# Moving the turn of the attention output one pipeline step later, and the score mask from the end of a step to just before its scores

## The chip, the cores and the metric

One core of a Trainium2 chip runs the whole program. The metric is the device time in microseconds (us), as the median of several runs; lower is better.

## The reference, cut to what matters

```python
x = x + L0(x, cond_512)   # modulated linear, attention over 16 heads within each token, modulated linear
x = x + L1(x, cond_512)   # low-rank linear map made from cond_512
x = x + L2(x, cond_512)   # modulated linear
x = x + L3(x, ids, cond)  # layer norms with gathered gains, six blocks through a 3072 -> 512 -> 512 MLP
```

`x` is 2 x 2048 tokens of 512 numbers. Only L0 is touched by the change:

```python
kx = modulated_linear(x, s, k_aff_w, k_aff_b, k_w, k_b).reshape(B, N, H, D)   # H = 16, D = 32
scores = einsum('bnhd,bnjd->bnhj', kx, kx) / sqrt(D)                          # 16 x 16 for each token
out = einsum('bnhj,bnjd->bnhd', softmax(scores), kx).reshape(B, N, F)
out = modulated_linear(out, s, o_aff_w, o_aff_b, o_w, o_b)
```

## The kernel before, in words

The 4096 tokens are 32 tiles of 128 (T = 32). L0 is a software pipeline: in step s each engine works on several tiles at once, in an order written out by hand in one function `attend(s, has)` for each engine; `has(k)` is true where tile s - k exists. `prepare(s)` follows each `attend(s)` and holds one-time work (weights, tables, low-rank factors). A list in `order` mixes the last steps (s from T to T + 7) with the first work of the later layers. All engines run their queues in order and wait on semaphores. `nth(MIX, "back", t + 1)` names a count of a semaphore that several links of one chain raise in turn: for the mixing chain "back" (VectorE), "styled" (GpSimd), "turned" (TensorE).

For tile t the work goes so:

- step t - 1: GpSimd multiplies the loaded tile by the style (`x_in`, L1668), ScalarE rounds it (`xh`, L1035), VectorE takes the rest (`xl`, L1324).
- step t: TensorE makes the keys in 12 products (`ps_k`, L663); VectorE scales (`kb`, L1298), GpSimd adds the bias (`kb`, L1685), VectorE turns 32 x 32 blocks (`kt`, L1309). At the end of its queue of step t + 1 TensorE writes a mask of large negative numbers into the score bank (`ps_s`, L681, one product of `mask_lr` and `mask_rr`, 128 rows of which two are not zero), for the tile whose scores come in the next step.
- step t + 1: ScalarE spreads the keys into a block diagonal (`k_diag`, L994).
- step t + 2: TensorE turns the keys into values (`ps_vt`, L634) and adds the scores onto the mask (`ps_s`, 32 products, L639). VectorE: `mx` (L1267), `low` (L1271); ScalarE `e` (L1021); VectorE `total` (L1287), `rinv` (L1291); GpSimd multiplies `e` by `rinv` (L1679); VectorE turns it into `at` (L1304); ScalarE spreads it (`at_diag`, L994).
- step t + 3: TensorE mixes the values (`ps_v`, L652, 32 products). VectorE turns the result into `om` (L1278) right after `low` of the next tile and before its `total`; GpSimd multiplies `om` by the second style (L1675); TensorE turns `om` at the end of its queue (`ps_t`, L702, 4 transposes).
- step t + 4: ScalarE rounds it at the head of its queue (`oh`, L1005, function `high_o`), VectorE takes the rest at the head of its own (`ol`, L1257, `low_o`), ahead of `mx`.

From step 8 on, TensorE makes one output block per step out of a finished group of four tiles (`ps_o`, 12 products, L604). SyncE loads its residual (`xb`, L468), GpSimd adds a bias to it (`xb`, L1662), VectorE adds the product (`xb`, L1319). In odd steps 5 to 19 TensorE also makes part of the decoder rows (`ps_u`, L691), in later steps table and fold products. GpSimd's order in a step is: residual bias, `x_in`, `om`, `e`, `kb`.

The wait of TensorE that both the old and the new order have ahead of the mixing product (before its first `ps_v` of a step) is:

```python
                    if later(t, 1):
                        pe.wait_ge(mix_step, nth(MIX, "back", t))
```

it holds the bank `ps_v` until VectorE has turned the tile before.

Of the kernel before, what the change touches and what calls it, by code (L numbers as in the profile page):

```python
# [5 lines left out]
F32 = mybir.dt.float32  # L6
F32R = mybir.dt.float32r
# [181 lines left out]
def body(nc, sems, I, A, M, ident, cond, style_t, demod_t, wv, table_t, u_dram, a_dram, x1_dram, out):  # L189
# [46 lines left out]
    with ExitStack() as ctx:  # L236
# [376 lines left out]
        def _(pe):  # L613
# [13 lines left out]
            def attend(s, has):  # L627
                if has(2):
                    t, p = s - 2, s % 2
                    pe.wait_ge(k_step, nth(KEYS, "turned", t + 1))  # L630
                    if later(t, 1):
                        pe.wait_ge(v_ready, t)
                    for m in range(PR // Q):
                        mm = nc.tensor.transpose(ps_vt[:, m, :], kt[p][:, Q * m:Q * m + Q, :].rearrange("p g h -> p (g h)"), ident[:, :])  # L634
                    mm.then_inc(v_turned, 1)
                    pe.wait_ge(k_diag_ready, t + 1)
                    for j in range(PR):
# [37 lines left out]
                if has(1):  # L675
                    if later(s, 2):
                        pe.wait_ge(softmax_step, nth(SOFTMAX, "low", s - 1))
                    else:
                        pe.wait_ge(mask_ready, 2)
                        pe.wait_ge(diag_zero, 3)  # L680
                    nc.tensor.matmul(ps_s[:, :, :], mask_lr[:, :], mask_rr[:, :], start=True, stop=False, skip_group_check=True)  # L681
# [12 lines left out]
                if has(3):  # L694
                    t = s - 3
# [286 lines left out]
        def _(act):  # L982
# [24 lines left out]
            def attend(s, has):  # L1007
                if has(4) and s != T + 3:
                    high_o(s - 4)
# [32 lines left out]
                if s == T + 2:  # L1042
                    high_o(T - 1)
# [179 lines left out]
        def _(dve):  # L1223
# [35 lines left out]
            def attend(s, has):  # L1259
                if has(4) and s != T + 3:  # L1260
                    low_o(s - 4)
# [63 lines left out]
                if s == T + 2:  # L1325
                    low_o(T - 1)
# [24 lines left out]
            def prepare(s):  # L1351
                m = slice(0, MLP_ROWS)
                if s == -1:
                    dve.wait_ge(consts_in, 16 * 4)
                    nc.vector.tensor_copy(mask_lr[0:2, :], at[0:2, 0:4, :].rearrange("p a b -> p (a b)")).then_inc(mask_ready, 1)
                    nc.vector.tensor_copy(mask_rr[0:2, :], e[0:2, :, :].rearrange("p a b -> p (a b)")).then_inc(mask_ready, 1)
# [290 lines left out]
        def _(pool):  # L1647
            nc.gpsimd.memset(mask_lr[:, :].bitcast(F32), 0.0)
            nc.gpsimd.memset(mask_rr[:, :].bitcast(F32), 0.0)
# [7 lines left out]
            def attend(s, has):  # L1657
                if has_o(s):
                    n = s - O_AT
                    fo = n % G  # L1660
                    pool.wait_ge(res_landed[n % 3], 16 * (n // 3 + 1))
                    nc.gpsimd.tensor_scalar(xb[n % 3][:, :], xb[n % 3][:, :], bias_o[:, fo:fo + 1], None, ALU.add).then_inc(xb_ready, 1)  # L1662
# [7 lines left out]
                if has(3):  # L1670
                    t = s - 3
                    pool.wait_ge(mix_step, nth(MIX, "back", t + 1))
                    if t == 0:
                        pool.wait_ge(style_bc_ready, B)
                    nc.gpsimd.tensor_tensor(om[:, :], om[:, :], bc[:, STYLE_O, t // TB, :], ALU.mult).then_inc(mix_step, 1)  # L1675
# [120 lines left out]
def program(nc, I, out):  # L1796
# [3 lines left out]
    with ExitStack() as ctx:  # L1800
# [31 lines left out]
        with ExitStack() as first:  # L1832
# [7 lines left out]
            A["mask_rr"] = sb1("mask_rr", [P, F], F32R)  # L1840
            A["mask_lr"] = sb1("mask_lr", [P, P], F32R)
# [150 lines left out]
```

## Time and profile before

| | |
|---|---|
| Median of 3 runs | 1030.34 us (1029.95 to 1034.31) |
| Profiled execution, its own time | 1029.95 us |
| Profiled execution, its span (first to last instruction) | 1028.2 us, mean granted TensorE clock 0.989 |
| Busy, share of the span | TensorE 95%, VectorE 65%, ScalarE 48%, GpSimd 68% |
| L0 (attention), with the first low-rank work beside its end | about 0 to 365 us |
| Later layers | about 365 to 1028 us |

Busy time is the sum over an engine's instructions with overlaps merged; the idle time ahead of an instruction is put down to what ended it.

### The profile page before, as it was taken

The numbers are of one execution on the slowest core, as the hardware profiler recorded it, in microseconds if no ns is written. First come the engines' busy times: TensorE is split into PE (matmuls) and PEld (weight loads), VectorE is DVE, ScalarE is ACT, GpSimd is POOL, SyncE is SP. The second block draws the span as 40 slices with busy tenths as digits, with TensorE's granted clock in tenths as the row PEclk, the third lists the DMA queues.
The fourth block names the chain that finished last, engine by engine and source line by source line (L and its number), as shares of the span: only waits on it lengthen the run. The fifth ranks groups of instructions, "written<-read, shape, count | busy, mean of one in ns | idle before, by whom it ended". The sixth has DMA issues, their size and how long they took to land.

```text
span 1028.2 us, 18103 instructions
## 1 busy us (share of the span) xinstructions
PE 977.9 (95%) x6546; PEld 779.9 (76%) x6546; DVE 667.1 (65%) x1213; ACT 489.8 (48%) x765; POOL 698.2 (68%) x634
## 2 busy tenths in 40 slices
PE   6978999999999796999999999999999999999995
PEld 4656777776787575888888887888888888888884
DVE  6786776678778667657557558666655656655542
ACT  2777778676777533434334325334333333332331
POOL 5546667585765348768768777777777777777861
PEclk9999999999999898999999999999999999999998
DMA  9634664554422454233233235124124215223220
GB/s 277 223 119 139 206 228 145 170 205 135 134 94 73 151 185 139 69 99 109 78 102 118 78 98 164 64 74 160 64 66 166 66 65 154 80 77 112 69 76 32
DMA packets 58270, 125.10 MB, mean 122 GB/s; under 512 B 7892, under 2 KB 12118, under 8 KB 57157
## 3 DMA queue, kind: packets, MB, share of 16 engines
q1 hardware_dynamic: 46404, 81.98, 23.9%
q0 software_dynamic: 11776, 41.95, 13.0%
q8 instruction: 53, 0.87, 0.4%
q14 instruction: 37, 0.30, 0.1%
HBM read 105.96 MB, written 17.95 MB: 121 GB/s over the span
## 4 chain that ended last, share of the span: by engine, by line
PE 63%; POOL 11%; issue 8%; DVE 8%; ACT 5%; DMA 2%; SPq 1%; POOLq 0%; DVEq 0%; ACTq 0%
PE ps L597 36%; PE ps_y L604 7%; PE tp L609 5%; PE ps_k L663 4%; PE ps_o L604 3%; DMA xb<-in_x_wide 2%; POOL om L1675 2%; ACT k_diag L994 2%; POOL e L1679 1%; ACT at_diag L994 1%; PE tp L898 1%; POOL kb L1685 1%; DVE mx L1267 1%; PE ps_s L639 1%; PE ps_v L652 1%
## 5 line engine op out<-in xcount | busy, mean ns | idle before, releaser
L1731 POOL TENSOR_TENSOR rstd<-var_eps,half 128x1 f32<-128x1 f32 x95 | 53.7, 566 | 106.7 <-DVE var_eps L1514 106.0
L1675 POOL TENSOR_TENSOR om<-om,bc 128x512 f32<-128x512 f32 x32 | 43.2, 1349 | 91.2 <-DVE om L1278 91.2
L1185 ACT ACTIVATE g_out<-ps 128x512 f32<-128x512 f32 x32 | 19.1, 598 | 172.0 <-PE ps L977 159.1
L994 ACT ACTIVATE at_diag<-at 32x512 f32<-32x512 f32 x128 | 80.4, 628 | 11.9 <-DVE at L1304 10.3
L1520 DVE TENSOR_SCALAR shift_n<-mean_var,rstd 128x1 f32<-128x1 f32 x96 | 20.6, 214 | 96.9 <-POOL rstd L1731 94.7
L994 ACT ACTIVATE k_diag<-kt 32x512 f32<-32x512 f32 x128 | 80.1, 626 | 1.1
L1662 POOL TENSOR_SCALAR xb<-xb,bias_o 128x512 f32<-128x512 f32 x32 | 51.6, 1613 | 38.4 <-DMA xb<-in_x_wide 38.3
L1126 ACT ACTIVATE h<-h,shift_n,rstd 128x512 f32<-128x512 f32 x32 | 26.1, 816 | 80.3 <-DVE shift_n L1520 80.3
L1500 DVE TENSOR_TENSOR t_lo<-tp,t_hi 128x512 fp32r<-128x512 f32 x64 | 43.8, 684 | 31.1 <-ACT t_hi L1122 31.1
L663 PE MATMUL ps_k<-wk_hi,xh 128*128 128x512 f32 x128 | 54.6, 427 | 0.7 <-DVE xl L1324 0.7
L1789 POOL DMA_INDIRECT path_rows<-in_path,pid x32 | 39.9, 1248 | 20.3 <-POOL pid L1777 20.3
L597 PE MATMUL ps<-wt_high,t_hi 128*128 128x512 f32 x128 | 53.1, 415 | 0.0
L597 PE MATMUL ps<-wx_high,x_hi 128*128 128x512 f32 x128 | 53.0, 414 | 0.0
L1764 POOL TENSOR_TENSOR o<-f,x3s 128x512 f32<-128x512 f32 x31 | 52.5, 1693 | 0.2
L1021 ACT ACTIVATE e<-low 128x512 f32<-128x512 f32 x32 | 20.2, 633 | 65.3 <-DVE low L1271 65.3
L597 PE MATMUL ps<-wout_high,g_hi 128*128 128x512 f32 x128 | 49.9, 390 | 1.4 <-DVE g_lo L1500 1.4
L604 PE MATMUL ps_y<-fh,w_high 128*128 128x512 f32 x128 | 50.5, 395 | 0.6 <-ACT y L1140 0.6
L663 PE MATMUL ps_k<-wk_lo,xh 128*128 128x512 f32 x128 | 51.0, 398 | 0.0
L604 PE MATMUL ps_o<-oh,wo_hi 128*128 128x512 f32 x128 | 50.3, 393 | 0.5 <-DVE xb L1319 0.5
L1753 POOL TENSOR_TENSOR tt<-xn,comp_rows 128x512 f32<-128x512 f32 x32 | 50.8, 1586 | 0.0
L604 PE MATMUL ps_y<-fl,w_high 128*128 128x512 f32 x128 | 50.7, 396 | 0.0
L663 PE MATMUL ps_k<-wk_hi,xl 128*128 128x512 f32 x128 | 50.7, 396 | 0.0
(293 smaller groups left out, 3223.4 us busy)
## 6 DMA issues: line engine op xcount, KB each, us to landing
raw<-in_dec_w SPq DMA_DIRECT2D x30, 512.0 KB, 5.3
x_in<-in_x_turned SPq DMA_DIRECT2D x32, 256.0 KB, 4.7
xb<-in_x_wide SPq DMA_DIRECT2D x32, 256.0 KB, 4.5
x_dram<-xb SPq DMA_DIRECT2D x32, 256.0 KB, 3.5
xt<-x_dram SPq DMA_DIRECT2D x8, 1024.0 KB, 8.3
out<-o SPq DMA_DIRECT2D x32, 256.0 KB, 2.0
raw<-in_int_W SPq DMA_DIRECT2D x7, 1024.0 KB, 6.0
id_rows<-in_id_rows SPq DMA_DIRECT2D x32, 64.0 KB
```

The costliest lines, as they stand in the source:

```text
L597: mm = nc.tensor.matmul(out_ps[:, :], x[:, c, :], w_[:, c, :], start=first and n == 0, stop=last and n == len(terms) - 1)
L604: mm = nc.tensor.matmul(out_ps[:, :], w_[:, c, at_], x[:, c], start=n == 0, stop=n == len(terms) - 1)
L609: mm = nc.tensor.transpose(bank[:, c, :], src[:, c * P:(c + 1) * P], ident[:, :])
L663: mm = nc.tensor.matmul(ps_k[:, :], x[:, c, :], w_[:, c, :], start=n == 0, stop=n == len(terms) - 1)
L994: last = nc.scalar.activation(dst[g, :, q, :], src[g, :, :], ACT.Copy)
L1500: nc.vector.tensor_tensor(lo[n][:, :, :], bank[:, :, :], hi[n][:, :, :].bitcast(F32), ALU.subtract).then_inc(lo_ready[n], 1)
L1662: nc.gpsimd.tensor_scalar(xb[n % 3][:, :], xb[n % 3][:, :], bias_o[:, fo:fo + 1], None, ALU.add).then_inc(xb_ready, 1)
L1675: nc.gpsimd.tensor_tensor(om[:, :], om[:, :], bc[:, STYLE_O, t // TB, :], ALU.mult).then_inc(mix_step, 1)
L1731: nc.gpsimd.tensor_tensor(rstd[:, k:k + 1], var_eps[:, k:k + 1], half[:, :], ALU.pow).then_inc(norm_step[k], 1)
L1753: nc.gpsimd.tensor_tensor(tt[:, :], xn[:, :], comp[:, F:2 * F], ALU.mult).then_inc(t_ready, 1)
L1764: nc.gpsimd.tensor_tensor(o[:, :], f2[:, :], x3s[f % 4][:, :], ALU.add).then_inc(o_ready, 1)
L1789: nc.gpsimd.indirect_dma_start(dst[:, :], None, I[table], bass.IndirectOffsetOnAxis(pid[:, k:k + 1], 0)).then_inc(landed, 16)
```

## The change

TensorE: the mask product moves from the end of step s - 1 to step s, between the turn of the values and the score products, with its waits; its operands shrink from 128 rows to 2. The turn of `om` (`ps_t`) is now that of tile s - 4 instead of s - 3, still at the end of the queue. ScalarE and VectorE: `oh` and `ol` are those of tile s - 5 instead of s - 4. VectorE: the turn of the mixed values into `om` (still tile s - 3) moves from between `low` and `total` to the end of `attend`, after `xl`. GpSimd: the multiplication of `om` is that of tile s - 4 instead of s - 3, and goes first; then `x_in`, then the residual bias, then `e`. Two memsets at GpSimd's start fall away.

```diff
 (TensorE, attend)
                     mm.then_inc(v_turned, 1)
                     pe.wait_ge(k_diag_ready, t + 1)
+                    if later(t, 1):
+                        pe.wait_ge(softmax_step, nth(SOFTMAX, "low", t))
+                    nc.tensor.matmul(ps_s[:, :, :], mask_lr[:, :], mask_rr[:, :], start=True, stop=False, skip_group_check=True)
                     for j in range(PR):
...
-                if has(1):
-                    if later(s, 2):
-                        pe.wait_ge(softmax_step, nth(SOFTMAX, "low", s - 1))
...
-                    nc.tensor.matmul(ps_s[:, :, :], mask_lr[:, :], mask_rr[:, :], start=True, stop=False, skip_group_check=True)
...
-                if has(3):
-                    t = s - 3
+                if has(4):
+                    t = s - 4
                     pe.wait_ge(mix_step, nth(MIX, "styled", t + 1))
...
 (ScalarE and VectorE, attend)
-                if has(4) and s != T + 3:
-                    high_o(s - 4)
+                if has(5) and s != T + 4:
+                    high_o(s - 5)
...
-                if s == T + 2:
+                if s == T + 3:
                     high_o(T - 1)
...
 (VectorE, attend, between "low" and "total")
-                if has(3):
-                    t = s - 3
-                    dve.wait_ge(mixed, t + 1)
-                    if later(t, 1):
-                        dve.wait_ge(mix_step, nth(MIX, "turned", t))
-                    nc.vector.transpose(om[:, :].rearrange("p (h a c) -> p h a c", h=H, c=2),
-                                        ps_v[:, :, :, :].rearrange("p a h c -> p h a c")).then_inc(mix_step, 1)
...
 (VectorE, attend, after xl: the same seven lines)
...
 (GpSimd, attend: new order)
+                if has(4):
+                    t = s - 4
+                    pool.wait_ge(mix_step, nth(MIX, "back", t + 1))
+                    if t == 0:
+                        pool.wait_ge(style_bc_ready, B)
+                    nc.gpsimd.tensor_tensor(om[:, :], om[:, :], bc[:, STYLE_O, t // TB, :], ALU.mult).then_inc(mix_step, 1)
                 if has(-1):
... (x_in, as before)
-                if has(3):
... (om of tile s - 3)
+                if has_o(s):
... (residual bias xb, as before)
                 if has(2):
... (e, as before)
...
-            A["mask_rr"] = sb1("mask_rr", [P, F], F32R)
-            A["mask_lr"] = sb1("mask_lr", [P, P], F32R)
+            A["mask_rr"] = sb1("mask_rr", [2, F], F32R)
+            A["mask_lr"] = sb1("mask_lr", [2, P], F32R)
```

## Rows read from the trace of the kernel before

**Rows 1.** Busy time by stretch: stretch, length, then PE, PEld, DVE, ACT, POOL, PEclk, DMA
```profile
0.00:370.00 370.00, 342.05 (x3455) 252.29 (x3456) 271.38 (x450) 256.46 (x421) 221.50 (x186) 0.99 0.50 163
...
420.00:1028.00 608.00, 594.99 (x2921) 494.93 (x2919) 358.68 (x717) 213.31 (x325) 440.61 (x421) 1.00 0.29 95
```

**Rows 2.** Waits of PE, 0 to 370 us: total, times, longest
```profile
PE ps_v L652 <- ACT at_diag L994: 9.8, 8, 2.1
PE ps_t L702 <- POOL om L1675: 8.6, 6, 4.5
```

**Rows 3.** Timeline of PE, 138 to 150 us: start, length, instruction
```profile
138.06 0.39 PE L681 MATMUL ps_s<-mask_rr,mask_lr 128*128 128x512 f32 x1
138.29 0.60 PE L702 MATMUL ps_t<-ident,om 128*128 128x128 f32 x4
...
139.25 1.08 PE L639 MATMUL ps_s<-k_diag,kt 128*32 128x128 f32 x32
140.15 1.06 PE L652 MATMUL ps_v<-at_diag,v 128*32 128x128 f32 x32
141.14 0.50 PE L663 MATMUL ps_k<-wk_hi,xh 128*128 128x512 f32 x1
...
149.91 1.08 PE L639 MATMUL ps_s<-k_diag,kt 128*32 128x128 f32 x32
```

**Rows 4.** Timelines of DVE and POOL over the same step, idle time before in brackets
```profile
138.93 0.68 DVE L1324 TENSOR_TENSOR xl<-x_in,xh 128x512 fp32r<-128x512 f32 x1
140.60 0.69 DVE L1257 TENSOR_TENSOR ol<-ps_t,oh 128x512 fp32r<-128x512 f32 x1 [0.99 <-ACT oh L1005]
...
141.93 0.69 DVE L1271 TENSOR_TENSOR low<-ps_s,mx 128x512 f32<-128x512 f32 x1
142.53 0.70 DVE L1278 STREAM_TRANSPOSE om<-ps_v 128x512 f32<-128x512 f32 x1
143.31 0.69 DVE L1287 TENSOR_REDUCE total<-e 128x16 f32<-128x512 f32 x1
...
144.58 1.05 POOL L1679 TENSOR_TENSOR e<-e,rinv 128x512 f32<-128x512 f32 x1
```

**Rows 5.** Timeline of ACT, 84 to 94 us
```profile
84.32 0.63 ACT L1021 ACTIVATE e<-low 128x512 f32<-128x512 f32 x1 [1.59 <-DVE low L1271]
...
93.31 0.63 ACT L1021 ACTIVATE e<-low 128x512 f32<-128x512 f32 x1 [1.59 <-DVE low L1271]
```

**Rows 6.** The instructions that write `om`: ns min/median/max, first and last start
```profile
L1675 POOL TENSOR_TENSOR om<-om,bc x32: 1262/1292/3216, 46.3 to 360.7; 128x512 f32<-128x512 f32 x32
```

**Rows 7.** Timelines of DVE and PE, 218 to 241 us
```profile
218.64 2.81 DVE L1324 TENSOR_TENSOR xl<-x_in,xh 128x512 fp32r<-128x512 f32 x1
...
220.71 1.06 PE L652 MATMUL ps_v<-at_diag,v 128*32 128x128 f32 x32
...
240.74 1.08 PE L652 MATMUL ps_v<-at_diag,v 128*32 128x128 f32 x32 [1.26 <-ACT at_diag L994]
```

**Rows 8.** Timeline of POOL, 92 to 98 us
```profile
92.64 1.58 POOL L1662 TENSOR_SCALAR xb<-xb,bias_o 128x512 f32<-128x512 f32 x1 [4.11 <-DMA xb<-in_x_wide]
...
96.44 1.05 POOL L1679 TENSOR_TENSOR e<-e,rinv 128x512 f32<-128x512 f32 x1
```

**Rows 9.** Timeline of POOL, 292 to 295 us
```profile
292.88 1.67 POOL L1721 TENSOR_TENSOR scale<-vareps,minus_half 128x8 f32<-128x8 f32 x1 [2.15 <-DVE vareps L1460]
```

**Rows 10.** Timelines at the end of the stage, DVE, POOL, ACT and PE
```profile
348.15 2.25 DVE L1545 TENSOR_TENSOR fl<-xt,fh 128x2048 fp32r<-128x2048 f32 x1
...
348.31 3.22 POOL L1675 TENSOR_TENSOR om<-om,bc 128x512 f32<-128x512 f32 x1 [5.78 <-DVE om L1278]
...
353.31 2.55 ACT L994 ACTIVATE at_diag<-at 32x512 f32<-32x512 f32 x4 [5.04 <-DVE at L1304]
...
351.58 1.11 PE L702 MATMUL ps_t<-ident,om 128*128 128x128 f32 x4 [4.50 <-POOL om L1675]
...
357.62 1.08 PE L652 MATMUL ps_v<-at_diag,v 128*32 128x128 f32 x32
```

More of the change, by code:

```diff
@@ L632, in attend @@
                         pe.wait_ge(v_ready, t)
+                    else:
+                        pe.wait_ge(mask_ready, 2)
+                        pe.wait_ge(diag_zero, 3)
                     for m in range(PR // Q):
@@ L1259, in attend @@
             def attend(s, has):
-                if has(4) and s != T + 3:
-                    low_o(s - 4)
+                if has(5) and s != T + 4:
+                    low_o(s - 5)
                 if has(2):
@@ L1324, in attend @@
                     nc.vector.tensor_tensor(xl[:, :, :], x_in[t % 2][:, :, :], xh[:, :, :].bitcast(F32), ALU.subtract).then_inc(xl_ready, 1)
-                if s == T + 2:
+                if has(3):
+                    t = s - 3
+                    dve.wait_ge(mixed, t + 1)
+                    if later(t, 1):
+                        dve.wait_ge(mix_step, nth(MIX, "turned", t))
+                    nc.vector.transpose(om[:, :].rearrange("p (h a c) -> p h a c", h=H, c=2),
+                                        ps_v[:, :, :, :].rearrange("p a h c -> p h a c")).then_inc(mix_step, 1)
+                if s == T + 3:
                     low_o(T - 1)
@@ L1354, in prepare @@
                     dve.wait_ge(consts_in, 16 * 4)
-                    nc.vector.tensor_copy(mask_lr[0:2, :], at[0:2, 0:4, :].rearrange("p a b -> p (a b)")).then_inc(mask_ready, 1)
-                    nc.vector.tensor_copy(mask_rr[0:2, :], e[0:2, :, :].rearrange("p a b -> p (a b)")).then_inc(mask_ready, 1)
+                    nc.vector.tensor_copy(mask_lr[:, :], at[0:2, 0:4, :].rearrange("p a b -> p (a b)")).then_inc(mask_ready, 1)
+                    nc.vector.tensor_copy(mask_rr[:, :], e[0:2, :, :].rearrange("p a b -> p (a b)")).then_inc(mask_ready, 1)
                     dve.wait_ge(squares_step, 3)
@@ L1647, in _ @@
         def _(pool):
-            nc.gpsimd.memset(mask_lr[:, :].bitcast(F32), 0.0)
-            nc.gpsimd.memset(mask_rr[:, :].bitcast(F32), 0.0)
             nc.gpsimd.memset(sq_wide[:, :, :], 0.0)
@@ L1657, in attend @@
             def attend(s, has):
[L1658 to L1662, printed above, removed]
+                if has(4):
[4 more added lines that the diff above has]
+                    nc.gpsimd.tensor_tensor(om[:, :], om[:, :], bc[:, STYLE_O, t // TB, :], ALU.mult).then_inc(mix_step, 1)
                 if has(-1):
@@ L1669, in attend @@
                                             style_t[:, 0, :, t // TB].unsqueeze(2).to_broadcast((P, C, P)), ALU.mult).then_inc(xm_ready, 1)
-                if has(3):
[L1671 to L1675, printed above, removed]
+                if has_o(s):
+                    n = s - O_AT
+                    fo = n % G
+                    pool.wait_ge(res_landed[n % 3], 16 * (n // 3 + 1))
+                    nc.gpsimd.tensor_scalar(xb[n % 3][:, :], xb[n % 3][:, :], bias_o[:, fo:fo + 1], None, ALU.add).then_inc(xb_ready, 1)
                 if has(2):
```

3 lines of the change are left out of this document (removed).

## The prediction, made before the changed kernel was timed

> **What bounds the kernel now.** I read the busy table first, then the waits of TensorE, then the timelines of single steps. The busy table by stretch [rows 1] says that TensorE is the bound almost everywhere: 594.99 of 608 us in the later layers, which the change doesn't touch, and 342.05 of 370 us in the attention stage. So the change can only earn TensorE's idle time in the first 370 us, 28 us, part of which is start-up. The waits of TensorE over that stretch [rows 2] name two that matter: 9.8 us in 8 waits for `at_diag` ahead of the mixing product, and 8.6 us in 6 waits for GpSimd's `om` ahead of the transposes, of which one alone is 4.5 us. The second kind is what the change takes away. Elsewhere the reader is to see one TensorE instruction starting while the one before still runs [rows 3]: a step with decoder rows goes from the scores at 139.25 to those at 149.91, 10.66 us of queued work without a gap.
>
> **The mask product.** It moves within TensorE's own queue and stays one product of 512 columns. Before, it cost 0.23 us (138.06 to the transposes at 138.29, rows 3). In its new place it stands between two kinds of products that read plain 4-byte data. The nearest row for such a switch is the first key product after the mixing products, 0.50 us long where the mask took 0.39 [rows 3], so 0.11 more. No row shows a two-row product. Bounds: no loss per step, as the same 512 columns stream through; against that twice the switch, 0.2 us, once in and once out. I take 0.1, one switch, in each step in which TensorE is the bound. These are some 19 of 32 steps (9 to 22 and 24 to 28): +1.9 us, bounds 0 and +3.8. Its wait, for `low` of the tile before, was over long ago in either place. The two memsets run while GpSimd waits for its first weights and cost nothing.
>
> **VectorE's turn of `om`.** In the old place it was almost free: `low` starts at 141.93, `total` at 143.31 [rows 4], and `total` needs ScalarE's `e`, which starts only when `low` is over and takes 0.63 us [rows 5]: 141.93 + 0.69 + 0.1 + 0.63 gives 143.35. So `total` gains nothing. In the new place it costs VectorE about 0.6 us (142.53 less 141.93 is the pace of such instructions) at the tail. The cover there is the idle time before `ol`, 0.99 us in this step [rows 4]. Where other work fills the tail, the cover is gone. What such a step gets back is that GpSimd's `e` no longer stands behind `om`, 1.29 us [rows 6]: it came 2.65 us after the start of `low` (144.58), and `total` ends at 144.0 with 0.25 for `rinv` after it, so it can come at 144.3, 0.25 earlier [rows 4]. A step with a full VectorE gets 0.6 - 0.25 = 0.35 us longer.
>
> **The new wait that this makes.** TensorE's mixing product waits for "back" of the tile before, which is this turn, and it is now the last thing VectorE does. In the bare step it would start 0.6 after `xl` at 138.93, so 139.53, and end 0.7 later, with the signal at 140.3; TensorE wants to start at 140.15 [rows 3, 4]. That is +0.15 in a bare step. The mask's 0.1 is inside it, so it adds 0.05 in the six bare steps: +0.3, bounds 0 and +0.9. Behind the mixing product stand the keys and the output block, for which VectorE waits in turn, so the stall lengthens the loop. In the step where `xl` takes 2.81 us (218.64 to 221.45, rows 7), the turn ends at 222.1 and the product that started at 220.71 stalls 1.3 us. That one is paid from idle time: at 240.74 TensorE waited 1.26 us anyway [rows 7].
>
> **The waits for `at_diag`.** They lie on a loop that the change leaves whole: ScalarE from one `e` to the next, 84.32 to 93.31, 8.99 us [rows 5], through `k_diag`, `xh`, `at_diag`, `oh`, then VectorE's `ol`, `mx`, `low`. `at_diag` starts when `xh` is done, not when `at` is. In steps 3 to 7 I find two with a full VectorE tail, one with 0.55 and one with 0.35: +0.9. In step 8 the change does help: GpSimd's residual bias waited for its load till 92.64 and then ran with `x_in` and `om` behind it, and `e` came only at 96.44, 3.8 us on [rows 8]. With `om` and `x_in` ahead of that wait, `e` can start when `rinv` is there, about 94.95; of the 1.49 us, 1.2 reach `at_diag`: -1.2.
>
> **The middle.** The steps up to 256 us are full of table work. VectorE starts them about 0.5 us less late than before, because a second late load of this kind, near 190 us, now holds up neither `om` nor `x_in`; with +0.35 for each of three steps this ends in +0.6 (bounds 0 and +1.4). At 292.88 GpSimd computes `scale` for 1.67 us after VectorE's tail [rows 9]. That tail is 0.6 later, and `om`, `x_in` and the residual bias, 3.8 us [rows 8], all stand between it and `e`; with its knock-on through the next full tail I take +1.0.
>
> **The end.** TensorE's turn of tile 30 waited 4.5 us because GpSimd's `om` took 3.22 instead of 1.29 us beside VectorE's 2.25 us `fl` [rows 6, 10]. This wait goes. What is late next is the same as before: `at_diag` of the last tile, 353.31 to 355.86, then the mixing product at 357.62 [rows 10], which today comes 1.7 us after it only because TensorE had its transposes and low-rank products still to do. With lags of 1.0 (from `scale`) and 1.05 (three full steps of 0.35), less 0.25 for the `e` before and 0.75 for the `fl` and `e` that come earlier, `at_diag` ends at 356.9: the mixing product is 0.7 us earlier. One turn more (0.5) now lies behind it, and the last of the six waits for `om` (some 0.4) is gone: -0.6 us at the end of the stage, with the +1.0 already in it.
>
> **Sum.** +1.9 + 0.3 + 0.9 - 1.2 + 0.6 - 0.6 = +1.9 us. The profiled execution took 1029.95 us by its own time (span 1028.2, the rest lies around it), 0.4 below the median of 1030.34. So 1031.9 us.
>
> **A rule weighed.** GpSimd's `om` beside `fl` [rows 10] was longer than its median [rows 6] by 1.9 us, nearly the length of the other. The Trainium skill, SBUF — State Buffer (the section on its doors), says that a VectorE instruction with two SBUF inputs and a GpSimd instruction that reads SBUF exclude each other for a whole instruction. By that rule, the trace agrees. What it would do here is rival (c).
>
> **The rivals.**
> (a) *The `om` waits are worth their full length.* For it: 8.6 us [rows 2], and the transposes after the longest took 1.11 us where they take 0.60 [rows 3, 10], so the 6 us of work up to 357.62 ran at about half pace: 3 us more. Against it: right behind each wait stands one for scores or `at_diag`, which moves with VectorE and ScalarE, not with TensorE. Time: 1029.95 - 8.6 - 3 + 1.9 = 1020.3.
> (b) *The new "back" wait decides; this ends slower.* For it: VectorE's signal at 140.3 against TensorE's 140.15, so no slack at all. If VectorE's tail is 0.3 us later than I think, for instance because `xl` is held now and then as in rows 7, the 19 steps pay it: 5.7 on top, 1037.6. At the length of a whole turn, 0.7, it would be 1045. It decides from 0.17 us a step (3.3 on top of 1.9). Against it: in steps with decoder or table rows TensorE has 1 to 2 us more to do before it comes to the mixing product.
> (c) *GpSimd becomes late.* Its `om`, `x_in` and residual bias, 3.8 us, all start now after VectorE's tail; from 140.3 they end at 144.1, and `e` wants to start at 144.3. An instruction held by 1.9 us as in rows 10 would use that up; in some seven full steps, about 1 us each after their own slack, +7: 1039. Against it: a full tail also puts off `e`.
> (d) *The mask gets cheaper by its two rows, or free.* Only its 0.23 us a step could go: 32 x 0.23 = 7.4 us, 1024.5. Against it: its columns are the same.
>
> **How the numbers follow.** Forecast 0.66; (a) 0.09; (b) 0.13; (c) 0.06; (d) 0.06. A measurement of this kernel tells about 0.5%, 5.2 us, from no change, that is 1025.2 to 1035.5. The bounds of the mask (-1.9, +1.9), of the bare steps (-0.3, +0.6), of the middle (-0.6, +0.8) and of the end (-3.5 if the lags don't arise, +1.5) give 1025.6 to 1036.7 for the forecast alone. To leave out no more than 2 in 10 I take 1023.5 to 1038, which has (d) and the milder half of (b) and (c), and none of (a). Faster: (a) and (d), 0.15. Slower: (b) and (c), with the forecast's upper end a little more than their mild ends, 0.20. Same: 0.65.
>
> **What would show it.** Right: no wait of TensorE for `om`; some short waits of `ps_v` for VectorE's `om`, one of over 1 us near 222 us; waits for `at_diag` still some 8 us; `at_diag` of step 8 about 1.2 us earlier; `total` at the same distance from `low`; the last mixing product near 359 us. Wrong: a step with decoder rows that is not 10.66 us plus 0 to 0.2; waits for `at_diag` that shrink below 5 us; the transposes at the end of the stage all at their usual 0.60 us; GpSimd's `e` starting well after `rinv`.

## The result, and the profile after

The changed kernel takes 1040.5 us in the median (1039.18 to 1043.8), the kernel before beside it 1030.34 (1029.62 to 1034.31): ratio 1.0094, 95% interval 1.0074 to 1.0114. The forecast was 1031.9, the range ended at 1038. The profiled execution took 1044.17 us by its own time, its span is 1042.4.

The waits of TensorE up to 380 us, the end of the attention stage in this kernel (total, times, longest):

```profile
...
PE ps_v L658 <- DVE om L1322: 5.1, 6, 1.9
PE ps_v L658 <- ACT at_diag L993: 3.8, 4, 1.6
PE ps_v L658 <- POOL om L1660: 3.2, 1, 3.2
PE ps_x L619 <- DVE wk_sq L1249: 3.1, 1, 3.1
PE ps_s L642 <- ACT k_diag L993: 2.7, 2, 1.7
```

The 8.6 us of `ps_t` for `om` [rows 2] are gone. In their place the mixing product `ps_v` waits for VectorE's turn. The third line names the wrong engine, as the timelines of the stage's end below show: by its code the product waits for `at_diag` and for VectorE's turn, which is over at 368.29. `at_diag` starts at 367.07 (353.31 before, rows 10), its four parts take 2.54 us (2.55 there) and end at 369.61, and the product starts at 369.67.

The step that answers to rows 3 and 4, a bare step (one without decoder rows), on TensorE and VectorE:

```profile
142.42 0.50 PE L642 MATMUL ps_s<-mask_rr,mask_lr 2*128 2x512 f32 x1
142.85 1.08 PE L645 MATMUL ps_s<-k_diag,kt 128*32 128x128 f32 x32
144.84 1.08 PE L658 MATMUL ps_v<-at_diag,v 128*32 128x128 f32 x32 [0.91 <-DVE om L1322]
```
```profile
131.55 0.68 DVE L1316 TENSOR_TENSOR xl<-x_in,xh 128x512 fp32r<-128x512 f32 x1
133.29 0.72 DVE L1322 STREAM_TRANSPOSE om<-ps_v 128x512 f32<-128x512 f32 x1 [1.06 <-PE ps_t L701]
133.93 0.39 DVE L1428 CAST v_parts<-v_rows 128x512 fp32r<-128x512 f32 x1
134.35 1.65 DVE L1430 TENSOR_TENSOR v_parts<-v_rows,v_parts 32x512 fp32r<-32x512 f32 x1
136.03 0.69 DVE L1256 TENSOR_TENSOR ol<-ps_t,oh 128x512 fp32r<-128x512 f32 x1
...
143.39 0.68 DVE L1316 TENSOR_TENSOR xl<-x_in,xh 128x512 fp32r<-128x512 f32 x1
143.99 0.71 DVE L1322 STREAM_TRANSPOSE om<-ps_v 128x512 f32<-128x512 f32 x1
```

Three things are to be seen. From the mask to the product behind it, it is now 0.43 us (0.23 before). The mixing product could start about 0.9 after the scores (rows 3: 139.25 to 140.15) and starts 1.99 after them, because the turn at 143.99 is still running. And the tail one step earlier is not just a turn longer: the turn waits 1.06 us for the transposes of the tile before, which share its one `om` buffer, and the second table instruction behind it takes 1.65 us where it took 0.68 before.

This step isn't the typical one. Two steps further on, without table work ahead of it, the mixing product starts 0.93 us after the scores, as good as without a stall (0.90 in rows 3). In the kernel with only the turn moved (e4 below, mask with 128 rows) it is 1.13 us:

```profile
163.69 1.08 PE L645 MATMUL ps_s<-k_diag,kt 128*32 128x128 f32 x32
164.62 0.64 PE L658 MATMUL ps_v<-at_diag,v 128*32 128x128 f32 x16
```
```profile
161.15 1.08 PE L639 MATMUL ps_s<-k_diag,kt 128*32 128x128 f32 x32
162.28 0.75 PE L652 MATMUL ps_v<-at_diag,v 128*32 128x128 f32 x20
```

The six waits of the first line of the table above are 0.82 us at 55.86, 0.31 at 103.69, 0.91 at 144.84, 0.82 at 228.04, 1.92 at 259.72 and 0.33 at 316.51. The three long ones after 140 us come behind a lengthened tail of VectorE: the table work at 134.35, an `xl` of 2.78 us at 224.49, and 4.0 us of table work at 246.99 to 251.00. In the last case VectorE is still late one step on, and its turn ends at 259.57.

The end of the stage, ACT, PE and PEld (TensorE's weight loads):

```profile
367.07 1.27 ACT L993 ACTIVATE at_diag<-at 32x512 f32<-32x512 f32 x2 [4.33 <-DVE at L1296]
```
```profile
369.67 1.25 PE L658 MATMUL ps_v<-at_diag,v 128*32 128x128 f32 x27 [3.20 <-POOL om L1660]
```
```profile
369.66 1.01 PEld L658 LDWEIGHTS ps_v<-at_diag,v 128*32 128x32 f32 x31 [3.64 <-ACT at_diag L993]
```

From tile to tile the lag of `at_diag` behind the kernel before is 2.6 us at tile 0 (it is anything from -0.6 to +2.2 in the kernels below, so I put it down to start-up and not to the change), 3.6 at tile 5, 2.7 at tile 9, 4.8 at 10, 5.2 at 15, 3.3 at 16, 8.7 at 24, 12.5 at 25 and 13.8 at 31. The first product of the residual stage is 14.06 late (379.69 against 365.63), and this lag stays to the end: spans 1042.4 and 1028.2. All the loss is made in the attention stage. It is spread over table steps and two jumps, at tiles 10 and 25. This is one execution against one; the medians differ by 10.2, not 14. The section on the jump at tile 25 gives a part of the difference.

Where VectorE is idle, 30 to 380 us, the kernel before first, then the changed one (waits by what ended them: total, times, longest):

```profile
DVE at L1304 <- POOL e L1679: 22.8, 25, 2.4
DVE ol L1257 <- ACT oh L1005: 18.9, 20, 1.7
...
DVE kb L1298 <- PE ps_k L663: 6.5, 10, 0.7
...
DVE mx L1267 <- PE ps_s L639: 2.9, 7, 0.9
...
DVE total L1287 <- ACT e L1021: 0.7, 1, 0.7
```
```profile
DVE total L1279 <- ACT e L1020: 21.6, 31, 0.7
...
DVE kb L1290 <- PE ps_k L669: 12.4, 18, 1.9
DVE at L1296 <- POOL e L1676: 12.0, 21, 1.2
DVE mx L1266 <- PE ps_s L645: 10.3, 10, 3.6
DVE ol L1256 <- ACT oh L1004: 5.2, 11, 0.8
DVE om L1322 <- PE ps_t L701: 5.0, 5, 1.1
```

The turn did stand in free time before: without it VectorE idles 21.6 us ahead of `total`. In the tail it finds as much cover: the idle time ahead of `at` and `ol` shrinks by 10.8 and 13.7 us. Added up, VectorE idles 20.9 us more ahead of `total` and 24.5 us less at the two other places, about even. What is new are waits for TensorE: 5.0 for the transposes, 5.9 more for the keys, 7.4 more for the scores. GpSimd isn't what is late: its `e` waits for VectorE's `rinv` 28 times in this stretch (42.5 us), where in the kernel before it did so once (0.6 us).

### The profile page after: what moved, and what is told of

It is laid out like the page before. It is cut to its first block, busy times and chain, and to the rows that moved or that the text cites. A ratio compares the mean times of both kernels' runs of the same rounds, so it can differ in the third digit from the quotient of the medians.

```text
span 1042.4 us, 18132 instructions
## 1 busy us (share of the span) xinstructions
PE 992.1 (95%) x6546; PEld 786.9 (75%) x6546; DVE 666.4 (64%) x1213; ACT 488.0 (47%) x765; POOL 701.2 (67%) x632
## 4 chain that ended last, share of the span: by engine, by line
PE 72%; POOL 8%; DVE 8%; issue 7%; ACT 3%; DMA 1%; SPq 0%; POOLq 0%; DVEq 0%; ACTq 0%
PE ps L597 36%; PE ps_y L604 7%; PE ps_k L669 7%; PE ps_o L604 5%; PE tp L609 5%; PE ps_v L658 2%; PE ps_s L645 1%; PE tp L897 1%; PE ps_u L690 1%; POOL kb L1682 1%; POOL e L1676 1%; PE ps_z L885 1%; DVE xl L1316 1%; ACT k_diag L993 1%; POOL h L1742 1%
## 5 line engine op out<-in xcount | busy, mean ns | idle before, releaser
L1660 POOL TENSOR_TENSOR om<-om,bc 128x512 f32<-128x512 f32 x32 | 48.1, 1502 | 81.4 <-DVE om L1322 81.4
L1676 POOL TENSOR_TENSOR e<-e,rinv 128x512 f32<-128x512 f32 x32 | 33.6, 1049 | 42.5 <-DVE rinv L1283 42.5
L669 PE MATMUL ps_k<-wk_hi,xh 128*128 128x512 f32 x128 | 56.8, 444 | 0.2 <-DVE xl L1316 0.2
L1786 POOL DMA_INDIRECT path_rows<-in_path,pid x32 | 39.9, 1248 | 20.3 <-POOL pid L1774 20.3
L669 PE MATMUL ps_k<-wk_hi,xl 128*128 128x512 f32 x128 | 52.8, 412 | 0.0
L597 PE MATMUL ps<-wt_high,t_lo 128*128 128x512 f32 x128 | 51.0, 398 | 0.0
```

Source lines behind the costliest of these rows:

```text
L597: mm = nc.tensor.matmul(out_ps[:, :], x[:, c, :], w_[:, c, :], start=first and n == 0, stop=last and n == len(terms) - 1)
L669: mm = nc.tensor.matmul(ps_k[:, :], x[:, c, :], w_[:, c, :], start=n == 0, stop=n == len(terms) - 1)
L1676: nc.gpsimd.tensor_tensor(e[:, :, :], e[:, :, :], rinv[:, :].unsqueeze(2).to_broadcast((P, PR, D)), ALU.mult).then_inc(softmax_step, 1)
L1786: nc.gpsimd.indirect_dma_start(dst[:, :], None, I[table], bass.IndirectOffsetOnAxis(pid[:, k:k + 1], 0)).then_inc(landed, 16)
```

## The experiments

There are 17 kernels; of the one with 64 rows (e8) only the trace is used. The effect in us is the ratio less 1, times 1032, the median of the kernel before beside most of them; in brackets its 95% interval. The letters of theories in the expectations are as they were put down then; B is that the turn's wait for the transposes makes the loss, V that VectorE's longer tail does.

| Run | Kernel | Median us | Ratio | Effect us |
|---|---|---|---|---|
| e1 | mask moved, 2 rows | 1035.05 | 1.0031 | +3.2 (2.0 to 4.5) |
| e2 | mask moved, 128 rows | 1031.54 | 0.9998 | -0.2 (-1.3 to 1.0) |
| e3 | mask in the old place, 2 rows | 1036.71 | 1.0044 | +4.5 (2.8 to 6.4) |
| e4 | only the turn moved | 1039.6 | 1.0068 | +7.0 (5.0 to 9.1) |
| e15 | changed kernel, mask with 128 rows | 1038.93 | 1.0071 | +7.3 (5.0 to 9.6) |
| e5 | turn moved, early transposes | 1044.62 | 1.0125 | +12.9 (11.4 to 14.3) |
| e17 | as e5, transposes late at the end | 1039.35 | 1.0083 | +8.6 (6.9 to 10.2) |
| e6 | turn moved, residual bias first | 1038.46 | 1.0066 | +6.8 (4.4 to 9.2) |
| e14 | turn moved, ahead of `xl` | 1041.38 | 1.0091 | +9.4 (7.1 to 11.8) |
| e11 | turn moved, behind the table work | 1053.56 | 1.0197 | +20.3 (17.8 to 23.0) |
| e7 | turn between `kb` and `at`, early transposes | 1037.35 | 1.0061 | +6.3 (4.3 to 8.3) |
| e10 | as e7, GpSimd's `om` first in its step, as in e5 | 1038.64 | 1.0057 | +5.9 (3.8 to 7.8) |
| e9 | as e7, transposes late at the end | 1034.35 | 1.0025 | +2.6 (1.1 to 4.0) |
| e16 | as e9, residual bias ahead of `x_in` | 1034.78 | 1.0021 | +2.2 (0.4 to 3.9) |
| e13 | before, an added instruction in the tail for which nobody waits | 1033.19 | 1.0010 | +1.0 (-0.4 to 2.5) |
| e12 | before, turn behind `kb`, `om` last | 1055.27 | 1.0213 | +22.0 (19.5 to 24.4) |

### The mask: place or rows

```diff
 # mask moved (on the kernel before); with [2, F] and [2, P] or with [P, F] and [P, P]
                     pe.wait_ge(k_diag_ready, t + 1)
+                    nc.tensor.matmul(ps_s[:, :, :], mask_lr[:, :], mask_rr[:, :], start=True, stop=False, ...)
...
-                if has(1):
-                    nc.tensor.matmul(ps_s[:, :, :], mask_lr[:, :], mask_rr[:, :], start=True, stop=False, ...)
 # two rows in the old place
-            A["mask_rr"] = sb1("mask_rr", [P, F], F32R)
+            A["mask_rr"] = sb1("mask_rr", [2, F], F32R)
```

> The kernel before, with only the mask product moved behind the value turns and cut to two rows; turn, output block and GpSimd's order as before. The trace of the changed kernel gives the mask 0.43 us in its new place against 0.23 before. Theory M (the mask is the main cost): 0.20 us in each of the 19 steps in which TensorE is the bound, +3.8 us, up to 6 us if further steps pay too: 1034 to 1036 us. Rival N (the loss comes from the VectorE turn in the tail and the new wait for it): 1030 to 1031 us, even if the mask's slot is 0.43 us, because then the loop through VectorE sets the pace. Rival H (the loss comes from more half-clock stretches): 1034 or more only if their total in the first 380 us grows from the 10 us of before; the trace tells.

> As the run with the mask moved, but the mask keeps its 128 rows, so that only the place differs from the kernel before. If the 0.20 us comes from the place (a product between two products of plain 4-byte data), the slot is 0.43 us here too and the time equals that of the two-row one within 0.5 us (theory M: 1034 to 1036). If it comes from the two rows, the slot is 0.23 us and the time that of the kernel before, 1030.

> The kernel before with the mask's operands cut to two rows, in the old place. Columns set the cost: slot 0.23 us, 1030 us. Rival (two rows are cheaper): up to 7.4 us less, 1023. Rival (two rows are dearer, by a switch of the array's shape): slot 0.3 to 0.43 us and 1032 to 1036.

> The kernel before with the mask's operands cut to 64 rows (two of them not zero), in the old place; read from the trace alone. With 2 rows the slot from the product before to the transposes behind was 0.74 us (0.32 + 0.42), with 128 rows 0.46. If any number of rows under 128 makes the weight load wait for the product before: 0.7 us again. If only few rows do (32 or fewer): 0.46 to 0.5 us.

The place costs nothing, the two rows cost 3.2 us in the new place and 4.5 in the old one. The slots say why. PE and PEld of the mask in the old place, with 2 rows:

```profile
140.26 0.39 PE L604 MATMUL ps_o<-ol,wo_hi 128*128 128x512 f32 x1
140.58 0.50 PE L681 MATMUL ps_s<-mask_rr,mask_lr 2*128 2x512 f32 x1
141.00 0.66 PE L702 MATMUL ps_t<-ident,om 128*128 128x128 f32 x4
```
```profile
140.58 0.18 PEld L681 LDWEIGHTS ps_s<-mask_rr,mask_lr 2*128 2x128 f32 x1 [0.35 <-issue]
141.00 0.42 PEld L702 LDWEIGHTS ps_t<-ident,om 128*128 128x128 f32 x4 [0.24 <-issue]
```

and in the kernel before the weight load alone:

```profile
137.84 0.19 PEld L681 LDWEIGHTS ps_s<-mask_rr,mask_lr 128*128 128x128 f32 x1
138.06 0.59 PEld L702 LDWEIGHTS ps_t<-ident,om 128*128 128x128 f32 x4
```

With 128 rows the mask's weights are loaded from 137.84, while the product before, which starts at 137.83, streams; the mask itself starts at 138.06. With 2 rows the load starts at 140.58, 0.32 us after the product before it and 0.35 us after the load before it ended. The next load, with 128 rows again, starts at 141.00, 0.42 us after the mask and 0.24 us after its load ended. That makes 0.32 + 0.42 = 0.74 us where it was 0.23 + 0.23. With 64 rows it is 0.32 + 0.43, read from its trace, so it is not the small number of rows:

```profile
140.31 0.50 PE L681 MATMUL ps_s<-mask_rr,mask_lr 64*128 64x512 f32 x1
140.74 0.66 PE L702 MATMUL ps_t<-ident,om 128*128 128x128 f32 x4
```

The Trainium skill, TensorEngine Tiling (Array Packing), Tiling Modes, Key Properties, says that changing the tiling mode drains TensorE; among its modes are ones of 64 and of 32 rows. The Trainium skill doesn't say that a plain product on 2 or 64 rows is such a change. The traces fit it, and no run here shows a drain as such: such a product, there and back, costs about 0.28 us in the old place. In the new place the product with 128 rows takes 0.36 + 0.41 us from the value turns to the scores (136.79, 137.15, 137.56), with 2 rows 0.53 + 0.43 (141.89, 142.42, 142.85, in the changed kernel): 0.19 more. Over 32 steps these slots would be 6.1 and 9.0 us; about half of it shows in the time.

### The moved turn: whole, and added to the mask

```diff
 # only the turn moved: the changed kernel with the mask in its old place and 128 rows
+                if has(1):
+                    nc.tensor.matmul(ps_s[:, :, :], mask_lr[:, :], mask_rr[:, :], start=True, stop=False, ...)
 # changed kernel, 128 rows: only
+            A["mask_rr"] = sb1("mask_rr", [P, F], F32R)
```

> The changed kernel with the mask put back to its old place with 128 rows, so that only VectorE's turn, the output block one step later and GpSimd's new order are left of the change. Theory M: what is left after +3.8 to +6 us for the mask, that is 1034.5 to 1036.5 us. Rival N (turn and its wait are all of the loss): 1040 us. Rival (the mask is all of it): 1030 us. Forecast by my own terms without the mask (0.3 + 0.9 - 1.2 + 0.6 - 0.6 = 0): 1030. Half-clock stretches in the first 380 us: about 24 us of them as in the changed kernel by rival H, about 10 us as before if the mask's place brings them on.

> The changed kernel with only the mask's two rows undone (128 rows, in the new place). The mask in its new place with 128 rows cost nothing on the kernel before, with two rows 3.2 us; the moved turn 7.0 us. If the parts add up: ratio to the kernel before 1.006 to 1.008, 1038 to 1040 us beside a kernel before of 1032. If they don't: 1.0094 as the changed kernel, or under 1.005.

The moved turn costs 7.0 us, with the mask in the new place and 128 rows 7.3. With the rows' 3.2 that makes 10.2, beside 9.7 (7.6 to 11.8) of the whole change: the parts add up within their intervals. In the trace of e4 the first product of the residual stage lags by 9.1 us.

### What of the turn costs: length, what it waits for, who waits for it

```diff
 # early transposes: ahead of the output block; late at the end: only in steps that make keys
+                if has(4):              # or: has(4) and has(0)
+                    for c in range(C):
+                        mm = nc.tensor.transpose(ps_t[:, c, :], om[:, c * P:(c + 1) * P], ident[:, :])
                 if has_o(s):
 # added instruction (on the kernel before), behind xl
+                    dve.wait_ge(softmax_step, nth(SOFTMAX, "at", s - 1))
+                    nc.vector.transpose(low_s[:, :, :], at[:, :, :])
 # turn between kb and at
                     nc.vector.tensor_tensor(kb[:, :], ps_k[:, :], ...)
+                    nc.vector.transpose(om[:, :]..., ps_v[:, :, :, :]...).then_inc(mix_step, 1)
                     nc.vector.transpose(at[:, :, :], e[:, :, :])
```

> The kernel with only the turn moved (128-row mask in the old place, 1039.6 us), with TensorE's transposes of om put right behind the keys' products instead of last in its step. In that kernel's trace VectorE's turn in the tail waits 6.5 us in 6 waits for TensorE's transposes of the tile before, as there is one om buffer, and TensorE's mixing product waits 7.5 us in 7 waits for that turn. Theory B (the single buffer makes the tail turn late, and the mixing product pays): with the transposes 3 to 5 us earlier in the step the turn's waits go (under 1 us), the mixing product's waits for it fall to 3 us or less, and the time falls by 2 to 4 us, to 1035.5 to 1037.5. Rival Q (the turn is late because it is queued last on VectorE, buffer or not): waits for the turn stay at 6 us or more and the time at 1039 to 1040. Rival G (GpSimd's new order is the cause): time unchanged as well, waits for the turn's buffer gone.

> The kernel with only the turn moved (1039.6 us), with TensorE's transposes behind the keys in the steps that make keys, and last as before in the last five. Theory B (the turn's wait for the transposes is most of the loss): 1033 to 1035.5 us. Theory W2 (most is the mixing product's wait for the turn and the work queued behind it on both engines, which stay in the tail): 1037.5 to 1039.5 us; the run with the turn between kb and at and the same order of TensorE took 1034.35. In the trace the waits of the mixing product for the turn should then stay near 8 us in some 11 waits, 0.5 to 0.75 us in each bare step, and those of the turn for the transposes go.

> The kernel before plus one added VectorE instruction per step behind xl, at the place to which the change moves the turn: a transposition of at into the tile of low, whose content is no longer needed there, 0.6 to 0.7 us, for which no engine waits. It measures a longer VectorE tail alone. Theory V (the length of the tail is the cost): 5 to 7 us, 1036 to 1039 us. Theory W (the wait of TensorE's mixing product for the turn is the cost, and the tail has cover before ol): 0 to 2 us, 1031 to 1034 us.

> A candidate for a better version. Transposes of om one step later and right behind the keys' products; VectorE's turn not in the tail but between its kb and at, where the kernel before idles 0.8 us in most steps (22.8 us in 25 waits for GpSimd's e); GpSimd's om last in its step, behind e and kb; mask as before. If the tail place is what costs (theories B and Q), the loss of the moved turn (7 us) goes: 1030 to 1033 us. If nothing waits for om any more and the 8.6 us of waits were worth something, 1026 to 1029. If the shift by one step itself costs, 1036 or more.

> The kernel with VectorE's turn between kb and at (1037.35 us), with one edit: in the steps without keys, the last five, TensorE's transposes stand last in the step again, behind the output block. In that kernel's trace the stage's last at_diag is 1.5 us later than in the kernel before, but the first product of the residual stage, ps_y, 5.95 us later, and the transposes wait 9.4 us in 5 waits for VectorE's ol. Theory E (its loss is mostly these waits in the last steps): waits for ol under 1 us, 3.5 to 4.5 us less, 1033 to 1034 us. Rival (the loss is that of table steps in the middle or of half-clock stretches): 1036 to 1037.5 us.

> The kernel with the early transposes (1044.6 us), with one edit: VectorE's turn stands between kb and at and not in the tail; GpSimd's order as there (om, x_in, bias, e, kb). It separates VectorE's tail from GpSimd's order. At the last at_diag of the stage the kernel with early transposes lags the one before by 6.9 us, the one with turn between kb and at and om last on GpSimd by 1.5 us. Theory V (the tail place on VectorE costs): lag 1 to 3 us, time 1037 to 1040 us. Rival G (om ahead of e on GpSimd costs): lag 5 us or more, 1043 to 1045 us.

The early transposes made it slower, not faster, because in the last steps they stood ahead of the output block and waited for `ol` (7.7 us in 4 waits). With them last again in those steps the kernel takes 1039.35 us, like the one with late transposes (1039.6).

The turn's wait for the transposes is gone from this trace, and nothing is won. That speaks against theory B, but it isn't a clean test of it. The transposes now stand ahead of the output block, and VectorE's `xb`, which stands ahead of the turn, waits for that block 5.6 us in 12 waits (1.6 in 1 before). The long stalls of the mixing product do shrink: it starts 1.57 us after the scores at 141.83 and 2.47 at 257.13, where it was 2.60 at 142.68 and 3.20 at 256.65. The plain steps get worse in return, 1.56 us instead of 1.13. What the wait for the transposes is worth by itself stays open.

The added instruction, 31 times 703 ns in the tail, costs 1.0 us (-0.4 to 2.5): as far as theory V says that the length of the tail is the cost, it falls.

With the turn between `kb` and `at`, and the same order of TensorE, the loss is 2.6 us instead of 8.6, and with the transposes early to the end 5.9 instead of 12.9: 6 to 7 us hang on the turn's place. The first of these pairs (e9, e17) also differs in whether GpSimd's `om` is last or first in its step, the second (e10, e5) does not; by e7 and e10 that is worth nothing that can be told (6.3 and 5.9). Nor is the first pair a matter of the clock: by their mean granted clocks, the timed runs of e9 and e17 spent 29.4 and 29.1 us at half clock. Those of e10 and e5 spent 33.2 and 39.1, which can make up to 3 of the 7 us of that pair.

Waits of PE, 0 to 380 us, with the turn in the tail and early transposes, late at the end:

```profile
PE ps_v L652 <- DVE om L1333: 8.2, 11, 1.4
```

and with the turn between `kb` and `at`:

```profile
PE ps_v L652 <- ACT at_diag L1004: 13.3, 8, 3.2
...
PE ps_k L663 <- DVE xl L1334: 1.5, 2, 0.8
...
PE ps_t L673 <- DVE ol L1267: 0.6, 1, 0.6
```

The first has a wait of 0.48 to 0.53 us in seven bare steps and of 1.02 to 1.39 in four others, as expected before it ran; the second has none for the turn, and more for `at_diag`.

### The place of the turn as a dose

```diff
 # ahead of xl; behind the table work: first instruction of the next step
+                if has(3):              # or, in the next step: has(4)
+                    nc.vector.transpose(om[:, :]..., ps_v[:, :, :, :]...).then_inc(mix_step, 1)
                 if has(-1):
                     nc.vector.tensor_tensor(xl[:, :, :], ...)
 # before, with the turn behind kb and GpSimd's om behind e and kb in the same step
                     nc.gpsimd.tensor_tensor(kb[:, :], kb[:, :], bias_k[:, :], ALU.add)
+                    nc.gpsimd.tensor_tensor(om[:, :], om[:, :], bc[:, STYLE_O, t // TB, :], ALU.mult)
 # residual bias first: ahead of om (e6) or of x_in (e16), and no longer behind them
+                    pool.wait_ge(res_landed[n % 3], 16 * (n // 3 + 1))
+                    nc.gpsimd.tensor_scalar(xb[n % 3][:, :], xb[n % 3][:, :], bias_o[:, fo:fo + 1], None, ALU.add)
```

> The kernel with only the turn moved (1039.6 us), with one edit: VectorE's turn stands behind the table work of the step (first in the next step, ahead of ol). At tile 10 the kernel with the turn moved loses 2.3 us: its turn waits 1.27 us for TensorE's transposes and the table work stands behind it, then ol. Theory B (that wait holds up what is queued behind): the jump at tile 10 shrinks to 1 us or less, but where the table work is long the mixing product waits longer for the turn: within 1.5 us of 1039.6 in sum. Theory V (each full tail pays the turn's 0.64 us wherever it stands in it): the 0.4 to 0.7 us per table step stay.

> The kernel with only the turn moved (1039.6 us), with VectorE's turn placed ahead of xl instead of behind it: the tail has the same length, the turn is 0.6 us earlier, and in the step of the 2.8 us xl some 3 us; in exchange xl and with it the keys are 0.6 us later. Theory W: waits of the mixing product for the turn fall from 7.5 to 4 us or less, and the time by 1 to 4 us, to 1036 to 1038.5. Theory V: 1039 to 1040 us. If it gets slower (1041 or more), xl for the keys is as tight as the turn.

> The kernel before, in which only VectorE's turn goes behind kb, ahead of at, and GpSimd's om behind e and kb in the same step; transposes, output block and mask as before. The turn should fill the 0.8 us in which VectorE waits for e, and GpSimd's e should start 0.3 us earlier. If a full VectorE step sets the pace: 0 to 0.1 us a step, 1029 to 1031 us. Against it, in bare steps om is ready about 1 us later, 0.4 us after TensorE wants its transposes: if that is on the path, up to 12 bare steps times 0.4, 1035 us.

> The kernel with only the turn moved (1039.6 us), with GpSimd's residual bias put back as the first of its step, ahead of om and x_in. Rival G (om and x_in ahead of the bias are what costs): about 1033 us. By my own forecast the new order saved 1.2 us at step 8, where the bias waits for its load: so 1 to 2 us longer than 1039.6, 1040.5 to 1041.5. Theory B and rival Q: within 1 us of 1039.6, as GpSimd waits over 2 us for om in most steps.

> The best version with the moved transposes so far (VectorE's turn between kb and at, transposes last in the steps without keys, 1034.35 us), with GpSimd's residual bias ahead of x_in as in the kernel before. At tile 19 that kernel loses 1.0 us, where xl takes 3.74 us beside GpSimd. If the order of x_in and bias decides how long xl is held: 1033 to 1033.5 us. Otherwise 1034 to 1035. Neither beats the kernel before by more than the measurement tells.

One place later, behind the table work, and the kernel loses 20.3 us instead of 7.0. The instruction is as long as before and stands in the same tail; what grows is TensorE's wait for it:

```profile
PE ps_v L652 <- DVE om L1265: 29.4, 17, 3.8
```

My expectation, within 1.5 us, was wrong by the size of this. One place earlier, ahead of `xl`, no wait of `ps_v` for the turn is left, but `at_diag` takes its place (13.3 us in 10 waits) and the turn waits 9.1 us for the transposes instead of 6.5, now with `xl` behind it: 9.4 us, about as bad. The kernel before with a turn 2 to 3 us later and the transposes in the same step is the dearest: TensorE waits 32.6 us in 25 waits for GpSimd's `om`, most of them in front of value turns and scores. I had counted 0.4 us for each of 12. The residual bias first changed nothing that can be told (6.8 against 7.0, 2.2 against 2.6); by my forecast it was to cost 1 to 2 us in the first kernel, and it could have gained 1 in the second.

### The jump at tile 25

In the trace with only the turn moved, three stretches with the granted clock behind PE, PEld, DVE, ACT and POOL:

```profile
284.00:287.00 3.00, 3.00 (x28) 2.45 (x20) 2.57 (x4) 2.94 (x5) 0.32 (x2) 0.97 0.17 62
287.00:293.80 6.80, 6.80 (x77) 5.66 (x77) 2.71 (x4) 1.91 (x5) 3.74 (x3) 0.51 0.27 92
293.80:297.00 3.20, 3.20 (x16) 2.61 (x15) 1.14 (x4) 2.38 (x4) 1.12 (x2) 1.00 0.00 0
```

For 6.8 us TensorE ran at half its clock (1.2 GHz of 2.4): the scores took 1.94 us instead of 1.08. It had not been idle before that; since 284.5 it ran products of two columns, 24 in all (`ps_x` from `u_row`, `v_rows`, `r_rows`). The kernel before runs the same products, and its profiled execution has the full clock there. From `at_diag` of tile 24 to that of tile 25 it is 9.99 to 10.46 us in the five profiled executions without such a stretch (before, e6, e7, e9, e15), 11.26 to 12.23 in six of the seven with 3.4 us of it (10.72 in e14), and 13.44 to 14.13 in the five with 6.8 us: the changed kernel (13.77) and e1, e4, e8, e16. (e11 and e12 have other waits there and are left out.) So about 3.5 us of the 14 between the two profiles go with this stretch (13.77 against 9.99 to 10.46 without it), which comes and goes with kernels that differ little. No experiment here switched it on or off by itself. Over all timed runs the mean clock gives 33.6 us at half speed for the changed kernel (14 runs), 28.5 for the one before (83 runs). The 5.1 us more (the standard error is 1.9) would be 2.5 us of the 9.7 if all of it was on the path. Among runs of one and the same kernel (221 runs in all), one us more at half clock goes with 0.22 us more time; by that it would be 1.1 us.

## Why the prediction was wrong

It was wrong by 8.6 us, and on the side of a rival. The terms without the mask added up to 0.0 us and measure +7.0 (5.0 to 9.1); the mask was put at +1.9 and measures +3.2 in its new place. Point by point:

**The mask.** I took +1.9 for its place, with bounds 0 and +3.8. Its place costs -0.2 (-1.3 to 1.0), its two rows +3.2. The upper bound was about right, the reason was not: "the same 512 columns stream through" is true, but the weight load no longer runs beside the product before it. Rival (d), cheaper by the rows, has the sign reversed: the rows cost 3.2 us instead of saving any. The Trainium skill's page cited above names a drain at a change of mode, and I had not weighed it.

**The new wait that this makes.** This is the step that failed. "the signal at 140.3; TensorE wants to start at 140.15 ... +0.3, bounds 0 and +0.9" was read from a single bare step of the old order and multiplied by six. For steps like that one it holds: the stall is 0.23 us with the mask of 128 rows (I had 0.15), and 0.03 with two rows, so that the mask's extra time is "inside it", as I had it. What failed is to price the wait by these steps alone. Where VectorE's tail was lengthened, in the same step or one before, the product stalls 0.8 to 1.9 us, 5.1 us in six waits in all, and the place of the turn is worth 6 to 7 us by four kernels in two pairs. I had seen that TensorE waits for the turn and that VectorE waits for TensorE. I had not drawn the conclusion that this closes a ring: mixing product, keys, `kb`, the rest of VectorE's queue down to `xl`, turn, next mixing product. On a ring, what doesn't fit in one round can return in the next. The waits on both sides show it (5.1 us of TensorE for the turn, 5.9 us more of VectorE for the keys); that it is all of the 6 to 7 us is argued, not shown.

That the turn also waits for the transposes of the tile before, in the same step, I had missed entirely; it shows (5.0 us in 5 waits), and what it is worth is open, as said above. The late `xl` of rows 7 was read rightly: the step with its stall is 1.2 us longer (scores to scores, 11.01 against 9.78), and the one that holds the old wait at 240.74 is 1.6 shorter (10.71 against 12.33). The stall that nothing paid for came after it, 1.92 us at 259.72.

**VectorE's turn.** Right in its sizes: `total` starts 1.38 us after `low`, as before, the turn takes most of the idle time before `ol` (18.9 us fall to 5.2), and the wait for `e` falls by 0.2 (0.82 to 0.62; I had 0.25). The added instruction (e13) confirms that length alone costs little.

**The waits for `at_diag`, and the step with the late load.** Right: from tile 0 to tile 5 the lag grows by 1.0 (I had 0.9), from tile 5 to tile 6 the changed kernel gains 1.3 us (I had 1.2), and from 15 to 16 it gains 1.9. But the waits of `ps_v` for `at_diag` fell from 9.8 to 3.8 us (7.0 with the one under GpSimd's name); I had said 8, and under 5 as a sign of being wrong.

**The middle and `scale`.** Undersized. I had +0.6 and +1.0; tiles 16 to 24 alone lose 5.4 us, of which the mask can be 1.5 (8 times 0.19). At tile 10 the turn's wait, the work behind it held to 1.65 us beside GpSimd's `om`, and the next stall of 0.91 come together, and the lag grows by 2.1. VectorE's collisions moved rather than grew: with only the turn moved, `v_parts` and `u_t` are 0.97 and 1.10 us longer, the three scalings of `raw` 0.82 us shorter each.

**The end.** Right that the 4.5 us wait was worth nothing by itself: the lag there goes from 13.8 at `at_diag` to 14.06 at the first residual product. "What is late next is the same as before: `at_diag`" holds, but the last mixing product comes at 369.67, where I had it near 359.

**The rivals.** (a) is refuted: all real waits for `om` are gone and the time is longer. (b) is what happened; its condition was a tail 0.3 us later in 19 steps, and the 7.0 us would be 0.37 in each, but they come in a few large pieces. I gave it 0.13. What I held against it, 1 to 2 us more of TensorE's work in steps with decoder rows, is so (no stall there), and wasn't enough. (c): GpSimd isn't late: its `e` waits for `rinv` in 28 steps, and the order of `om` and of the residual bias changes nothing that can be told (e7 and e10, e4 and e6). In the stage, with only the turn moved, its `om` take 4.9 us more in sum and its `x_in` 3.3 less. (d) is answered under the mask.

Two things stay open. The shift by one step with the turn in a harmless place still costs 2.6 us (1.1 to 4.0), and I didn't find where. And the share of the half-clock stretches is estimated at 1.1 to 2.5 us of the 9.7, not shown. No version here beats the kernel before.

## What to carry to other kernels

If a moved instruction is waited for by the engine that feeds it, lay out two rounds of the ring with the new order before calling its cost small: an instruction for which nobody waits cost 1.0 us in that place, this one 6 to 7. A slack read in a plain step of the old order says nothing of the steps in which the queue ahead is longer. A wait that is taken away is worth its length only if nothing else ends at the same time; look at what the next product waits for. Cutting a small operand to the rows that it needs can cost more than it saves, where its neighbours use all 128.

## What the runs showed of the hardware that was not expected

- A product of 2 or 64 rows between products of 128 costs 0.28 us more than one of 128 rows (0.19 in the other place). Its weight load starts 0.32 us after the product before it, where it is 0.01 us with 128 rows.
- 24 products of two columns each were followed, in 13 of the 19 profiled executions by 3.4 or 6.8 us at half clock, though TensorE was busy throughout; with 6.8 us of it the step is about 3.5 us longer (13.44 to 14.13 against 9.99 to 10.46).
- A wait for several signals was put down to GpSimd's `om` (3.2 us) where `at_diag` ended 0.06 us before the product started.
